# Attention sums of exponentials as two f16 parts, their matmuls at key tile 2, one projection at key tile 0

## The reference

```python
scores = jnp.einsum('bhqd,bhkd->bhqk', q, k)
scores = scores + position_bias
attn = jax.nn.softmax(scores.astype(jnp.float32), axis=-1).astype(scores.dtype)
out = jnp.einsum('bhqk,bhkd->bhqd', attn, v)
out = out.transpose(0, 2, 1, 3).reshape(b, s, INNER)
return out @ wo
```

## Time and profile before

| | |
|---|---|
| Time, median of 3 runs | 2971.9 us (2971.86 to 2973.07) |
| Time of the profiled execution | 2971.88 us |
| Its span in the profile | 2970.1 us |
| PE busy | 2836.7 us, 96% |
| POOL busy | 2275.2 us, 77% |
| DVE busy | 1836.8 us, 62% |
| ACT busy | 1672.6 us, 56% |

### The profile page before, as it was taken

One profiled execution on the slowest core, in us unless ns is written; L12 is line 12 of the kernel. 1 busy time (PEld: TensorE's weight loads), 2 busy tenths in 40 slices (PEclk: granted clock), 3 DMA queues, 4 the chain that ended last, 5 costly groups with the idle time before them and its releaser, 6 DMA issues.

```text
span 2970.1 us, 49731 instructions
## 1 busy us (share of the span) xinstructions
PE 2836.7 (96%) x18785; PEld 1048.1 (35%) x18785; DVE 1836.8 (62%) x4663; ACT 1672.6 (56%) x2182; POOL 2275.2 (77%) x1033
## 2 busy tenths in 40 slices
PE   5999999999999999999999999999999999988997
PEld 2333333333333333333333333333333333322443
DVE  7556655665656665665655566655665566685666
ACT  4555565555555555555555555555555555556576
POOL 0788888888888888988888898888888888977000
PEclk9999999999999999999999999999999999999999
DMA  5000000000000000000000000000000000100001
GB/s 158 19 1 1 1 19 1 1 1 2 19 2 1 1 19 2 1 1 19 1 1 1 1 19 1 2 1 19 1 1 1 1 9 2 58 1 29 1 1 57
DMA packets 45137, 35.73 MB, mean 12 GB/s; under 512 B 21554, under 2 KB 43314, under 8 KB 44898
## 3 DMA queue, kind: packets, MB, share of 16 engines
q1 hardware_dynamic: 44898, 32.56, 3.8%
HBM read 27.60 MB, written 10.55 MB: 13 GB/s over the span
## 4 chain that ended last, share of the span: by engine, by line
PE 50%; DVE 23%; issue 20%; ACT 4%; POOL 3%; DMA 0%; SPq 0%; DVEq 0%; ACTq 0%; POOLq 0%
PE po L633 17%; PE st L603 15%; PE pre L615 5%; DVE mpart L1330 4%; PE pm L570 4%; DVE st L1347 3%; DVE pre L1327 3%; PE st L869 3%; POOL acc L541 3%; DVE pre L1322 2%; PE pm L576 2%; PE pm L663 2%; ACT prob L959 1%; PE pm L642 1%; DVE y L1381 1%
## 5 line engine op out<-in xcount | busy, mean ns | idle before, releaser
L541 POOL TENSOR_TENSOR acc<-acc,prob 128x1024 f32<-128x1024 f32 x896 | 2115.9, 2361 | 383.2 <-ACT prob L959 303.3
L959 ACT ACTIVATE prob<-st 128x1024 f32<-128x1024 f32 x1024 | 1016.5, 1021 | 914.8 <-DVE st L1347 814.3
L633 PE MATMUL po<-prob,v 128*64 128x512 f32 x4096 | 994.8, 606 | 0.0
L603 PE MATMUL st<-qk 64*128 64x512 f16 x6144 | 836.0, 378 | 18.0 <-ACT prob L959 16.1
L1322 DVE CUSTOM_DVE_ANT_0 pre<-pre,ew 128x512 f32<-128x512 f32 x448 | 300.8, 713 | 560.4 <-issue 560.3
L1327 DVE CUSTOM_DVE_ANT_0 pre<-pre,tab 128x512 f32<-128x512 f32 x704 | 475.2, 715 | 144.2 <-issue 144.2
L603 PEld LDWEIGHTS st<-qk 64*128 64x128 f16 x6144 | 293.6, 95 | 346.5 <-ACT prob L959 58.9
L633 PEld LDWEIGHTS po<-prob,v 128*64 128x64 f32 x4096 | 248.8, 136 | 440.8 <-issue 364.6
L603 PE MATMUL st<-eq,ek 64*128 64x512 f16 x2048 | 390.0, 377 | 0.0
L615 PE MATMUL pre<-qk 64*128 64x512 f16 x1600 | 309.5, 384 | 38.4 <-ACT ew L989 16.5
L1330 DVE TENSOR_REDUCE mpart<-pre 128x2 f32<-128x1024 f32 x224 | 274.0, 1223 | 97.9 <-PE pre L615 96.2
(11 more groups left out here) (204 smaller groups left out, 2325.4 us busy)
## 6 DMA issues: line engine op xcount, KB each, us to landing
t_scratch<-w_scratch SPq DMA_DIRECT2D x2, 2688.0 KB
inv_r<-inv SPq DMA_DIRECT2D x260, 1.0 KB, 1.7
qk<-x SPq DMA_DIRECT2D x8, 512.0 KB, 5.6
out<-qk SPq DMA_DIRECT2D x8, 512.0 KB, 3.6
w<-w_pairs SPq DMA_DIRECT2D x8, 384.0 KB, 3.9
t2f<-t_scratch SPq DMA_DIRECT2D x8, 384.0 KB, 4.8
t<-t_scratch SPq DMA_DIRECT2D x8, 384.0 KB, 3.2
den_c<-den_s SPq DMA_DIRECT2D x130, 2.0 KB, 1.7
```

Of the source, the lines that this page charges most:

```text
L541: nc.gpsimd.tensor_tensor(acc[g % 2][:, :, :], a, prob[:, n % RING, :, :], ALU.add).then_inc(sum_p, 1)
L603: last = nc.tensor.matmul(st[:, 2 * (n % 2) + h, :], w[64 * h:64 * h + 64, :], t[64 * h:64 * h + 64, :], start=(r == 0), stop=(r == len(te ...
L633: last = nc.tensor.matmul(po[64 * h:64 * h + 64, :], v[:, g // CHUNKS, j, 64 * h:64 * h + 64], prob[:, n % RING, h, :], start=(s == 0), st ...
L959: nc.scalar.activation(prob[:, n % RING, :, :], st[:, 2 * (n % 2):2 * (n % 2) + 2, :], ACT.Exp).then_inc(exp_done, 1)
```

## The change

1. The sums are split into two f16 parts before `den`. ACT copies `acc` of the chunk before to `acc16[:, 0]` (`high_sums`, in `rest(0)`, after the exponentials of steps 2 and 3). POOL subtracts that from `acc` into `acc16[:, 1]` (`low_sums`, after its addition of step 1). `acc16` lies in a part of `ew16`, so the profile calls it `ew`.
2. `den` multiplies both parts with an f16 constant: four f16 matmuls in place of two f32 ones (each f32 one leaves two records). It stands at step 2 instead of step 1.
3. The projection of step 2 moves to step 0. In the last pair one transpose moves from step 2 to step 1. The sums after the last chunk keep their f32 matmuls.
4. POOL's first addition of a chunk waits for its own `low_sums` of the chunk before instead of for `den`.

```diff
-JOBS = {1: ("den", 0), 2: ("proj", 0), 4: ("proj", 1), 6: ("proj", 2), 8: ("inv", 0), 11: ("max", 0), 12: ("y", 0), 14: ("y", 1),
+JOBS = {0: ("proj", 0), 2: ("den", 0), 4: ("proj", 1), 6: ("proj", 2), 8: ("inv", 0), 11: ("max", 0), 12: ("y", 0), 14: ("y", 1),
         15: ("proj", 3)}
-INV_AT, REST_AT, HIGH_AT, LOW_AT = 4, 6, 9, 10
+SUMS_AT, INV_AT, REST_AT, HIGH_AT, LOW_AT = 1, 4, 6, 9, 10
...
+            def low_sums(G, g):
+                pool.wait_ge(acc_hi, G + 1)
+                nc.gpsimd.tensor_tensor(acc16[:, 1, :, :], acc[(g + 1) % 2][:, :, :], acc16[:, 0, :, :], ALU.subtract).then_inc(acc_lo, 1)
...
                     if s == 1:
-                        pool.wait_ge(den_ready, G + 1)
+                        pool.wait_ge(acc_lo, G)
                         a = prob[:, (n - 1) % RING, :, :]
...
+                    if s == SUMS_AT:
+                        low_sums(G, g)
                     if s == REST_AT:
                         rest_of_inverse(G)
...
+            def denominators(G):
+                pe.wait_ge(acc_lo, G + 1)
+                for n in range(2):
+                    for h in range(2):
+                        last = nc.tensor.matmul(pm[64 * h:64 * h + 64, :], unit16[:, :], acc16[:, n, h, :], start=(n == 0), stop=(n == 1))
+                last.then_inc(den_ready, 1)
...
+            def high_sums(G, g):
+                act.wait_ge(sum_p, (G + 1) * SUMS)
+                act.wait_ge(den_ready, G + 1)
+                nc.scalar.activation(acc16[:, 0, :, :], acc[(g + 1) % 2][:, :, :], ACT.Copy).then_inc(acc_hi, 1)
...
+                    if s == 0:
+                        high_sums(G, g)
```

More of the change, by code:

```diff
@@ L86 @@
 FIRST_SCORES = 3
-TR_AT = [(6, 13), (6, 15), (7, 0), (7, 2), (7, 3), (7, 4), (7, 5), (7, 6)]
+TR_AT = [(6, 13), (6, 15), (7, 0), (7, 1), (7, 3), (7, 4), (7, 5), (7, 6)]
 SQ = 16
@@ L232, in layer @@
         unit = sb("unit", [128, 64], f32)
+        unit16 = sb("unit16", [128, 64], f16)
         t1 = sb("t1", [128, 2, BAND], f32)
@@ L269, in layer @@
         kd = ew16[:, 0, 1, :].rearrange("p (b n k) -> p b n k", b=B, n=2)
+        acc16 = ew16[:, 1, 0, :].rearrange("p (n h q) -> p n h q", n=2, h=2)
         ewh, ewl = ew16[:, 0, :, :], ew16[:, 1, :, :]
@@ L329, in layer @@
         sum_p = sem("sum_p")
+        acc_hi = sem("acc_hi")
+        acc_lo = sem("acc_lo")
         den_ready = sem("den_ready")
@@ L520, in _ @@
             nc.gpsimd.memset(unit[:, :], 1.0 / INV_UNIT).then_inc(set_pool, 1)
+            nc.gpsimd.memset(unit16[:, :], 1.0 / INV_UNIT).then_inc(set_pool, 1)
             nc.gpsimd.memset(wo16[:, :, :], 0.0).then_inc(wo_lo, 1)
@@ L635, in values, with last_denominators @@
                 last.then_inc(pv_done, 1)
-            def denominators(G, g):
+            def denominators(G):
[4 more added lines that the diff above has]
+                last.then_inc(den_ready, 1)
+            def last_denominators(G, g):
                 pe.wait_ge(sum_p, (G + 1) * SUMS)
@@ L751, in _ @@
                 piece(1, 1, u)
-            pe.wait_ge(set_pool, 2)
+            pe.wait_ge(set_pool, 3)
             pe.wait_ge(set_v, 15)
@@ L798, in jobs @@
                         elif kind == "den":
-                            denominators(G, g)
+                            denominators(G)
                         elif kind == "inv":
@@ L824, in _ @@
             pe.wait_ge(y_add, G_ALL * YJ + 1)
-            denominators(G_ALL, 0)
+            last_denominators(G_ALL, 0)
             def back(b, t):
```

## The result

The changed kernel takes 3113.98 us (median of 4 runs, 3113.42 to 3115.84), against 2972.06 us before on the same chip: a ratio of 1.0478, with a 95% interval from 1.0462 to 1.0494. It is 142 us slower; 108 us slower was forecast, and 3114 lies within the range.

The account below looks back on a forecast made before the run. PE's list was taken to bound the kernel. Losses of 43 us with projections and 75 us without, less 8 us for vanished waits, made 110 us on 2971.88: about 3080 us, own range 3055 to 3110, stated range 3025 to 3125.

Parts of the forecast that it names:

- What bounds the kernel: Attention stage: PE, busy 96% of the span, sets the time; a new wait of PE is not made up later.
- What PE saves: Sums on PE: 0.53 us in f16 against 0.86 us in f32, saving 0.33 us a chunk if nothing waits.
- The price of the subtraction: POOL's subtraction for the second f16 part: taken as 2.36 us, as for the same number of elements in f32.
- The rival of a much dearer subtraction: POOL's subtraction costs double through its mixed types, 2.36 us more in 62 chunks: 3228 us; chance 0.08.
- Step 2, chunks with projections: PE waits at the sums, behind POOL or DVE; about 0.95 us lost in each of 45 chunks, 43 us.
- the 8 us that the prediction took back for vanished waits: PE idles about 4 us in a pair; one of them was assumed to vanish in the new waits, 8 us.
- hidden, or nearly: Step 8, chunks with projections: the inverse, usable at T0 (start of a chunk's second piece) + 23.1, against PE there at 23.2.
- DVE's way round: Step 2: projection's copy behind ACT's new copy, then DVE's low part and piece, delaying PE's sums to T0 + 7.2.
- Step 8, chunks without projections: PE waits for the late inverse until T0 + 23.1 instead of 18.7; 4.4 us lost in each of 17 chunks, 75 us.
- f16 matmuls that don't run side by side: Rival at the sums: the two heads' matmuls run in turn, 0.43 us more in 45 chunks: 3101 us; chance 0.10.
- That only step 2 waits: Rival: the inverse comes sooner, so chunks without projections lose only 1.6 us, at step 2: 3034 us; chance 0.14.
- That POOL's part is too short to be waited for: Faster rival: POOL's work is much shorter than its rows say, so PE keeps its saving: 2951 us; chance 0.05.

Follow-up runs that it names:

- e10: The kernel before, with only the remainder of the inverse on POOL moved after its addition of step 7 instead of 6: 3004.54 us, ratio 1.0108.
- e3: The kernel before, with only the table of jobs changed (projection at step 0, still f32 sums at step 2): 2985.44 us, ratio 1.0045.
- e9: Changed kernel: ACT's copy before step 3's exponential, inverse's remainder after step 5, wo's low part at step 3, f32 sums at step 1 in last pair's chunks 4-7: 2961.72 us.
- e1: The changed kernel, with the remainder of the inverse on POOL after its addition of step 4 instead of step 6: 3045.18 us, ratio 1.0246.
- e2: The changed kernel, with 12 extra f16 matmuls on PE ahead of the wait for the inverse in 19 chunks: 3095.98 us, ratio 1.0416.
- e6: The changed kernel without POOL's subtraction; PE multiplies only ACT's f16 copy, so the sums are rounded to f16: 2992.89 us, ratio 1.0067.

## Why the prediction came out as it did

**What bounds the kernel** held. PE's list is the time: a wait put into it is not made up (e10), unless a later wait was there to take it in (e3), and 0.4 us taken out of it in most chunks is kept (e9).

**What PE saves** held, and was a little undersized: the f16 sums take 0.45 us (1361.61 to 1362.06), not 0.53, so 0.41 instead of 0.33 us a chunk. The heads' f16 matmuls run side by side, and that rival falls.

**The price of the subtraction** was taken as 2.36 us and is 2.13 us, 0.23 us less. The rule of the Trainium skill that the prediction weighed against it (GPSIMD Engine Reference, "Elementwise — side-by-side cycle accounting") gave an estimate of 2.2 us and was nearer. What the prediction drew from it, that a narrower output doesn't help, is not borne out: the subtraction takes 10% less than the f32 additions of 2367 ns, though one of its inputs is f16 too, and no run tells the two apart. The rival of a much dearer subtraction falls.

**Step 2, chunks with projections**: the sums were put at T0 + 7.2 and 6.8. They start at T0 + 7.1 and 7.3 in chunks 5, 0 and 4, and at 6.5 in chunks 2 and 6. Missed was chunk 1, at 8.3: DVE's low part of wo, 1.25 us, stands in the rest of step 1, right behind the projection's low part, and I had not looked for what else is in that rest. Over the chunks with projections the loss comes to 0.5 to 0.6 us and 1.8 us in chunk 1, about 35 us, where 43 were forecast.

Two things under that sum differ from the forecast. In chunks 0, 1, 4 and 5 the values of step 2 are late by 0.8 to 1.1 us (2.1 in chunk 1), but 0.3 to 0.5 us of that are an old wait that is gone, some 13 us over the kernel; the 8 us that the prediction took back for vanished waits were a guess of the right kind. In chunks 2 and 6 the values are only 0.2 us late, and the 0.6 us is lost at step 8: before, PE was there at T0 + 22.0, and now the inverse can be used only at 22.6. The prediction called step 8 hidden, or nearly, for all chunks with projections, after working it out for chunk 5. In e1, where the inverse is early, these chunks lose 0.2 us. (A slip of its sum for DVE's way round: 4.3 + 0.59 is 4.9, not 4.8; the copy ended at T0 + 4.6.)

**Step 8, chunks without projections**: forecast T0 + 23.1 and a loss of 4.4 us; measured T0 + 22.6 to 23.3 and 4.1 to 4.4 us. 17 x 4.2 is 72 us, where 75 were forecast. e10 makes a wait of this kind from the kernel before, and e1 takes it away. What these chunks lose at step 2 was put down to POOL alone, 1.6 us; it is 1.2 us, and most of PE's idle time there is the wait for ACT's `rise_of_piece` behind the new copy. Since step 8 decides, this did not touch the sum.

**The term that was missing** is the clock. The prediction read a granted clock of 1.00 in the pair before and took it over as given. The new idle time changed it. 42 us more of full-speed time are not granted, 34 of them between 102 and 2600 us, where PE works nearly without pause and pays for it. 72 + 35 us of waits and about 35 us of clock are the 142 us. e2 shows that the clock follows from idle time: filled with useless matmuls, the longest wait costs less.

The clock also means that the range held by luck. The forecast's own range ended at 3110 us, below the measured 3114. The last 15 us of the stated range were there for a rival, f16 matmuls that don't run side by side, and that did not happen.

**The rivals.** That only step 2 waits is refuted by the timeline. That POOL's part is too short to be waited for is refuted by the group's 2126 ns and by e6, which takes the low part away and with it 121 us. The share of the move alone is 13 us (e3).

Left open: what chunk 3 and the last pair lose in e9, and which waits the clock answers to and which not.

## What to carry to other kernels

When work is added for an engine that has time to spare, ask for the moment at which its input is there, and what stands behind it in the queue, rather than for its share of the span: here POOL idled 4.1 us in each chunk while it was what everything waited for, and moving one copy ahead of one exponential was worth 103 of 142 us. A path over several engines and a queue of DMAs that shows no wait may still have no room; one step of it made later (e10) tells how much it has, here 0.6 to 0.7 us. And where PE works without pause, price idle time twice: once for its length and once for the clock behind it.

## What was not expected of the hardware

Waits of 1 to 3.6 us, spread over a stage in which PE is otherwise busy, lowered the granted clock from 1.00 to half for a few microseconds behind some of them, in 16 places between 102 and 2600 us: 0.56 in the window from 1463.40 to 1467.30 us, with the eight matmuls of the values taking 3.32 instead of 1.94 us. The mean clock of the whole execution went from 0.989 to 0.976, and with e2's twelve useless matmuls in 19 chunks it was 0.985. In e10 one wait of 1.8 us out of the fourteen in the first seven pairs was followed by such a stretch. POOL's subtraction of f32 and f16 into f16 took 2126 ns, 10% less than the addition of f32 to f32 of the same size, 2367 ns.
